# A second place for the indices: loaded a block ahead and copied by GpSimd in a recommender-tower kernel

## The reference

```
e = stack([tbl_f[ids[:, f]] for f in range(39)], axis=1)      # 1024 x 39 x 16, fp32
x0 = xk = e
for layer (W, b) in (w0, b0), (w1, b1), (w2, b2):             # 128 units each
    z = einsum('bhd,bkd,hks->bsd', x0, xk, W) + b
    z = relu(z)
    if layer is not the last: xk = z[:, :64]; direct.append(z[:, 64:])
    else: direct.append(z)
logit = sum(concatenate(direct, axis=1), axis=-1)             # 1024 x 256
h = relu([logit, dense_ctx] @ W_top1 + b_top1)
h = relu(h @ W_top2 + b_top2)
y = h @ W_top3                                                # 1024 x 1
```

## Time and profile before

| | value |
|---|---|
| median of 3 runs | 1287.43 us (1285.81 to 1289.83) |
| the profiled execution: time, span | 1289.77 us, 1287.9 us |
| mean granted TensorE clock | 0.989 of full speed |
| busy: PE, DVE, POOL, ACT | 95%, 89%, 71%, 55% |
| DMA moved | 233.58 MB, mean 181 GB/s |
| share of the chain of waits that `DMA idx<-in_ids` has | 7% |

### The profile page before, as it was taken

One profiled execution on the slowest core, in us unless ns is written; L12 is line 12 of the kernel. 1 busy time (PEld: TensorE's weight loads), 2 busy tenths in 40 slices (PEclk: granted clock), 3 DMA queues, 4 the chain that ended last, 5 costly groups with the idle time before them and its releaser, 6 DMA issues.

```text
span 1287.9 us, 15315 instructions
## 1 busy us (share of the span) xinstructions
PE 1227.4 (95%) x4114; PEld 778.7 (60%) x4114; DVE 1140.8 (89%) x1025; ACT 704.6 (55%) x739; POOL 909.2 (71%) x573
## 2 busy tenths in 40 slices
PE   0599999999999999999999999999999999999999
PEld 0345656666566666666666666666666666666654
DVE  1258999999999999999999999999999999999990
ACT  0234655566555655656555555666556565565552
POOL 7677778786878778787778778787778755555440
PEclk9979999999999999999999999999999999999999
DMA  7198878889878888898888888898778888898500
GB/s 187 26 226 192 193 191 193 196 199 220 185 171 187 196 198 193 202 218 207 169 187 191 197 198 197 204 220 194 171 185 197 196 200 199 203 218 188 133 28 0
DMA packets 134646, 233.58 MB, mean 181 GB/s; under 512 B 16546, under 2 KB 23827, under 8 KB 134513
## 3 DMA queue, kind: packets, MB, share of 16 engines
q1 hardware_dynamic: 83165, 151.03, 51.3%
q10 hardware_dynamic: 41474, 79.71, 24.4%
q0 software_dynamic: 9984, 2.58, 2.0%
HBM read 229.39 MB, written 6.23 MB: 183 GB/s over the span
## 4 chain that ended last, share of the span: by engine, by line
PE 74%; DMA 9%; DVE 7%; issue 4%; POOL 4%; SPq 1%; ACT 0%; DVEq 0%; POOLq 0%; ACTq 0%
PE z_odd L920 29%; PE z_even L920 27%; PE z_even L954 8%; DMA idx<-in_ids 7%; PE z_odd L954 4%; DVE whole L764 4%; POOL gathered L503 2%; DMA x_shift<-x_rows 2%; DVE whole_psum L764 2%; DVE rest L797 2%; PE whole_psum L948 1%; POOL rest L516 1%; SPq L458 1%; PE x_odd L974 1%; PE z_odd L888 1%
## 5 line engine op out<-in xcount | busy, mean ns | idle before, releaser
L516 POOL TENSOR_TENSOR rest<-whole,head 128x1024 fp32r<-128x1024 f32 x256 | 611.4, 2400 | 255.6 <-ACT head L621 232.1
L764 DVE TENSOR_TENSOR whole<-x_banks,x_rep 128x1024 f32<-128x1024 f32 x448 | 533.9, 1216 | 41.5 <-ACT x_banks L579 33.1
L503 POOL DMA_INDIRECT gathered<-in_tbl,idx x312 | 297.2, 953 | 91.6 <-issue 77.8
L621 ACT CAST head<-whole 128x1024 fp32r<-128x1024 f32 x256 | 268.6, 1049 | 151.7 <-DVE whole L764 96.7
L621 ACT CAST head<-whole_psum 128x1024 fp32r<-128x1024 f32 x192 | 194.9, 1015 | 139.6 <-DVE whole_psum L764 126.5
L764 DVE TENSOR_TENSOR whole_psum<-x_banks,x_rep 128x1024 f32<-128x1024 f32 x192 | 235.5, 1226 | 6.0 <-DMA x_rep<-x_rows 3.9
L797 DVE TENSOR_TENSOR rest<-whole_psum,head 128x1024 fp32r<-128x1024 f32 x192 | 234.6, 1222 | 0.6 <-ACT head L621 0.6
L920 PE MATMUL z_odd<-head,w_rest 128*128 128x512 f32 x427 | 197.6, 463 | 9.0 <-POOL rest L516 9.0
L920 PE MATMUL z_even<-head,w_rest 128*128 128x512 f32 x405 | 186.2, 460 | 0.0
L920 PE MATMUL z_odd<-whole,w_whole 128*128 128x512 f32 x400 | 185.2, 592 | 0.5 <-issue 0.5
L920 PE MATMUL z_odd<-head,w_head 128*128 128x512 f32 x460 | 181.7, 395 | 0.0
(11 more groups left out here) (93 smaller groups left out, 960.9 us busy)
## 6 DMA issues: line engine op xcount, KB each, us to landing
x_rep<-x_rows ACTq DMA_DIRECT2D x128, 512.0 KB
x_rep<-x_rows SPq DMA_DIRECT2D x128, 512.0 KB
x_shift<-x_rows SPq DMA_DIRECT2D x93, 546.0 KB
x_rep<-x_rows ACTq DMA_DIRECT2D x32, 384.0 KB
x_rep<-x_rows SPq DMA_DIRECT2D x32, 384.0 KB
x_rep<-x_rows SPq DMA_DIRECT2D x32, 256.0 KB
gathered<-in_tbl,idx POOLq DMA_INDIRECT x312
x_rows<-xt_and_ctx SPq DMA_DIRECT2D x32, 78.0 KB
```

Source lines behind the costliest of these rows:

```text
L503: nc.gpsimd.indirect_dma_start(gathered[:, f, :], None, tables[f], bass.IndirectOffsetOnAxis(ap=idx[:, f:f + 1], axis=0)).then_inc(s_gathe ...
L516: nc.gpsimd.tensor_tensor(rest[:, split_slot(product)], whole_slot(product), head[:, split_slot(product)].bitcast(F32), ALU.subtract).then ...
L621: nc.scalar.copy(head[:, split_slot(product)], src).then_inc(s_head, 1)
L764: nc.vector.tensor_tensor(out[0:rows, 0:width, :], xk[0:rows, :].unsqueeze(1).to_broadcast([rows, width, N]), x0, ALU.mult).then_inc(s_pro ...
```

## The change

The index tile gets a second place, `idx_next`. SP loads `idx_next` and no longer `idx`, and GpSimd copies `idx_next` to `idx`.

- At the start SP loads block 0 into `idx` and, right behind it, block 1 into `idx_next`.
- SP's further loads (`load_indices`) stand in steps with t % 4 = 3, at the same place of the step. They wait for the semaphore of the copy that emptied `idx_next`, and no longer for `s_emb`.
- In steps with t % 4 = 2 GpSimd waits, ahead of the rest of j = 7 of layer 1, for `s_emb` and for the load of `idx_next`; behind that rest it copies 128x39 numbers; ahead of the rest of j = 9 it waits for its own copy. The eight gathers behind j = 9 stay.
- Before the early gathers GpSimd waits for `s_emb` and the load, copies, and waits for the copy.
- SP's loop has five turns and no longer six, the others' loops six as before.

```diff
+        idx_next = sb("idx_next", [P, FIELDS], I32)
         idx = sb("idx", [P, FIELDS], I32)
...
-            sp.dma_start(idx[:], by_block[0]).then_inc(s_idx, 16)
-
-            def next_indices(t):
-
-                done = t.plus(AHEAD).blocks(1, 1)
-                if t.first % TPB == TPB - AHEAD and (t.turn is not None or done < BLOCKS):
-                    sp.wait_ge(s_emb, done)
-                    rows = by_block[done] if t.turn is None else by_block[bass.ds(done, 1)]
-                    sp.dma_start(idx[:], rows).then_inc(s_idx, 16)
+            sp.dma_start(idx[:], by_block[0]).then_inc(s_ids0, 16)
+            sp.dma_start(idx_next[:], by_block[1]).then_inc(s_ids, 16)
+
+            def load_indices(t):
+
+                copied = t.plus(1).blocks(1, 1)
+                if t.first % TPB == TPB - 1 and (t.turn is not None or copied + 1 < BLOCKS):
+                    sp.wait_ge(s_idx, copied)
+                    rows = by_block[copied + 1] if t.turn is None else by_block[bass.ds(copied + 1, 1)]
+                    sp.dma_start(idx_next[:], rows).then_inc(s_ids, 16)
...
-                next_indices(t)
+                load_indices(t)
...
-            steps(sp, body, TURNS - 1)
+            steps(sp, body, TURNS - 2)
...
+            def copy_indices():
+
+                nc.gpsimd.tensor_copy(idx[:], idx_next[:]).then_inc(s_idx, 1)
...
-                    if j == split[-1] and refill is not None:
-                        refill()
-                        refill = None
+                    if refill is not None and j == split[-2]:
+                        pool.wait_ge(s_emb, refill)
+                        pool.wait_ge(s_ids, refill * 16)
+                    if refill is not None and j == split[-1]:
+                        pool.wait_ge(s_idx, refill)
                     pool.wait_ge(s_head, before(t, layer, j, "PV") + 1)
                     nc.gpsimd.tensor_tensor(rest[:, split_slot(product)], whole_slot(product),
                                             head[:, split_slot(product)].bitcast(F32),
                                             ALU.subtract).then_inc(s_rest_p, 1)
+                    if refill is not None and j == split[-2]:
+                        copy_indices()
+                    if j == split[-1]:
+                        refill = None
...
-            pool.wait_ge(s_idx, 16)
+            pool.wait_ge(s_ids0, 16)
...
-            pool.wait_ge(s_idx, 32)
+            pool.wait_ge(s_emb, 1)
+            pool.wait_ge(s_ids, 16)
+            copy_indices()
+            pool.wait_ge(s_idx, 1)
...
-                        def refill():
-
-                            pool.wait_ge(s_idx, ahead.blocks(16, 32))
+                        refill = ahead.blocks(1, 1)
```

More of the change, by code:

```diff
@@ L212, in build_kernel @@
         s_select = sem("first_shift_selected")
-        s_idx = sem("idx_loaded")
+        s_ids0 = sem("first_ids_loaded")
+        s_ids = sem("next_ids_loaded")
+        s_idx = sem("idx_ready")
         s_gather = [sem(f"gather_landed_{g}") for g in range(len(GATHER_GROUPS))]
```

## The result

The changed kernel took 1281.14 us (median of 6 runs, 1277.37 to 1282.03), the kernel before 1287.39 us (6 runs, 1285.24 to 1291.23). The measured ratio, which is not the quotient of these two medians (0.9951), is 0.9946, with a 95% interval of 0.993 to 0.9963: faster, by 0.37% to 0.70%, or 4.8 to 9.0 us. The profiled execution took 1281.85 us (span 1280.0). A second measurement on another occasion gave the same ratio, 0.9945. A third, told under the last experiments, did not: its ratio was 1.0062, and over half of the executions took 18 to 31 us more than the fastest one. (Ratios leave out runs far above a kernel's fastest; ranges and medians keep them.)

The account below looks back on a forecast made before the run. TensorE was held by GpSimd rests waiting for late index loads. Savings of 9.90 us less 0.4 at the start gave 1280.3 from the profiled 1289.77; allowing for that execution standing above the median, 1278.5, range 1275.5 to 1283.0.

Parts of the forecast that it names:

- The wait and its place: GpSimd's index-load wait ahead of the rest of j = 9 delays TensorE in six steps; stalls together 7.08 us.
- The 9.90 us of stalls, refills and clock: Savings in steps 2 to 22: stalls 6.96 us, five refills 1.30, step 6's clock 1.64.
- In hand 0.60 us: Step 14: the rest of j = 9 was 1.36 us late, TensorE stalled 0.76, so it had 0.60 in hand.
- refill 0.26: TensorE's extra time after each stall in the windows of four tiles, 0.26 us a stall.
- The cover: Step 14: GpSimd's 1.49 us idle before j = 9's head plus 0.60 in hand, 2.09 us until TensorE notices.
- The copy: GpSimd's 128x39 copy behind the rest of j = 7, taken at 0.4 us with semaphore waits, hidden by the cover.
- Rival 1: A copy of 2.5 us with waits leaves 2.7 us of stalls; 5.6 us off, about 1282; chance 0.10.
- rival 4: Copy with its waits takes more than today's 3.25 us of GpSimd idle; time 1291.5; chance 0.05.
- rival 3: Only the first copy is slow, 6 us, stalling step 0; net 2 us, 1280.5; chance 0.05.
- Rival 2: The later index transfer delays `x_shift` or `x_rep` loads and DVE waits, 1.2 us a block; about 1287; chance 0.10.
- The sum of the profiled pair: Whole kernel: 9.90 less 0.4 at the start, 9.5 us off the profiled 1289.77, giving 1280.3.
- I take 0.4 us: Start: SP's third-block load in step -1 delays tile 1's `x_shift`; cost 0.4 us, from nothing up to 1.0.

Follow-up runs that it names:

- wait_behind_rest: The kernel before with only its index-load wait moved behind the rest of j = 9, GpSimd's loop written out; 1280.22 us, ratio 0.995.
- start_part_only: The changed kernel's start, but from step 2 on the loads and the wait of the kernel before; 1289.85 us against 1288.66, ratio 1.0009.
- six_more_copies: The changed kernel with six further waited-for 128x39 copies ahead of the real one in steps 2 to 22, GpSimd's steps written out; 1288.02 us, ratio 0.9989.
- steady_part_only: The changed kernel with the start of the kernel before, third block's load in step 0; 1280.96 us, ratio 0.9954.

## Why the prediction came out as it did

The forecast was 1278.5, range 1275.5 to 1283.0; measured 1281.14, faster, on the right side and inside the range.

*The wait and its place* were right: wait_behind_rest and start_part_only show from both sides that holding the rest of j = 9 was the cost.

*The 9.90 us of stalls, refills and clock* were right in size: 9.98 by the table. The clock part is seen in one pair of traces (granted clock 0.81 before, 1.00 after in step 6). In start_part_only, with the waits back, step 6 took 38.35 and step 7 an undisturbed 36.15. So the drop does not come in every execution, as the prediction left open; how much of it the median of the kernel before carries is not known.

*"In hand 0.60 us" and "refill 0.26"* were one thing. The steps grew by the lateness of the rest less 0.34 to 0.38: 1.98, 1.87, 1.36, 1.18 and 1.74 us late in steps 2, 10, 14, 18 and 22 gave steps longer by 1.60, 1.52, 1.02, 0.83 and 1.38. With 0.39 us late, six_more_copies grew by 0.06 to 0.09. So a step grows from about 0.35 us of lateness on and not from 0.60. The cover was 1.8 us, not 2.09. For a copy of 0.22 us this changed nothing.

*The copy*, taken at 0.4 us with its waits, took 0.22 us, its first use included (0.21 at 55.89). That first copy began 0.06 us after the `emb` copy for which it waited. The Trainium skill (GPSIMD Engine Reference, section Instruction dispatch) gives about 6 us for loading code at the first call to a freshly loaded kernel; the trace shows no such time at this copy.

*Rival 1 and rival 4* (a dear copy) fell with that, *rival 3* (a slow first copy) too. *Rival 2* (time given back elsewhere) is not seen in the changed kernel's traces: from step 2 to 29 every step is at 36.14 to 36.17 but step 6 (36.32) in one of three profiles, and DVE's waits for `x_rep` sum to 3.8 us in that one, against 5.0 before.

*The sum of the profiled pair.* 7.9 us came off where the sum had 9.5. The steady terms held (9.98 for 9.90). What was missing is the start (1.08 for 0.4) and two things that the sum had at nothing: the pace, some 0.5, and 0.4 after step 30. The pace goes with the kernel. Every profile of a kernel made from the changed one has steps 27 to 29 at 36.14 to 36.17; wait_behind_rest, made from the kernel before, has them at 36.13. Why is open.

*The start, "I take 0.4 us"*, is the term that is least settled. The profiled pair lost 1.08 us up to step 1, but steady_part_only, with the old start, had the same median as the changed kernel. What the start takes varies by itself: over the undisturbed profiles of kernels without these stalls step 1 began anywhere from 138.44 to 143.84. What differs between them is when the clock came back in step -1 and what then waited, GpSimd's gathers or `x_shift`. And the third occasion showed a loss of 9 to 31 us, against that occasion's fastest execution, that no term of the sum had.

*The size as a median*: forecast 8.9 us off, measured 6.25, with 4.8 to 9.0 by the interval. That the median came so near the forecast is in part luck: the start's spread of 5 us hides where in the interval the value lies.

## What to carry to other kernels

When an engine's only idle time of note sits in front of one instruction, look first whether the wait belongs to that instruction at all. Here the rest did not need the indices, only the gathers behind it did, and moving the wait down by one instruction gave the same gain without a buffer, and left the start of the kernel as it was. Count a stall by the lateness at the consumer, less what the consumer has in hand, and compare step lengths rather than idle rows: they hold stall and refill in one number. When a kernel of a test has to be written in another form, such as steps written out instead of looped, take a profile of the form alone. And when a change starts work earlier, measure it on more than one occasion, even if the steady part can't be affected.

## What was not expected of the hardware

- A GpSimd copy of 128x39 int32 takes 0.21 to 0.23 us, and a chain of six, each waiting for the one before, 0.27 us apiece.
- A stall of 2.04 us in one execution was followed by a granted clock of 0.81 over the next 9 us; stalls of 1.93 us in another (start_part_only, step 6) and of 1.91 were not.
- In two profiles of one occasion ACT's first copy behind TensorE's transposes came 25 and 28 us late, 1.7 and 3.8 us after GpSimd had issued its last early gather. All other engines were idle meanwhile and the DMA engines nearly so (DMA share 0.05 to 0.08).
- In five of five profiles of kernels with GpSimd's steps written out and SP's looped, 2.9 to 6.4 us were lost in scattered steps where DVE waited for `x_rep` loads; in nine profiles of the other forms at most 0.2 us. The cause is open.
